# Casting all weights to bf16 ahead, and loading four of them from SyncE's queue instead of GpSimd's

## The reference, cut to what is computed

```python
def outer(x, Wq, bq, Wk, bk, Wv, bv, Wo, bo):     # x: (4, 4096, 1024), 16 heads of 64
    summary = ...                                 # mean of each 64 tokens: 64 rows a batch
    q = x @ Wq + bq; k = summary @ Wk + bk; v = summary @ Wv + bv
    attn = softmax(where(64*c <= t, q @ k.T / 8, -inf))
    return (attn @ v) @ Wo + bo

def inner_layer(x, wqkv, qs, ks, wo, lg, lb, w1, b1, w2, b2):   # 8 heads of 64, window 512
    q, k, v = split(shift_token(x) @ wqkv, 3)     # wqkv: 1024 x 1536
    q, k = rotary(l2norm(q) * qs, l2norm(k) * ks)
    x = x + local_attention(q, k, v) @ wo         # wo: 512 x 1024
    h = layernorm(shift_token(x)) * lg + lb
    a, g = split(h @ w1 + b1, 2)                  # w1: 1024 x 5460
    return x + (a * gelu(g)) @ w2 + b2            # w2: 2730 x 1024

x = x + outer(layernorm(x), ...)
x = x + inner(layernorm(x), ...)                  # inner: two inner_layers, one after the other
```

## Time and profile before

| | us |
|---|---|
| median of 3 runs | 9315.27 |
| lowest, highest | 9222.44, 9327.99 |
| the profiled execution | 9222.44 |
| its span, slowest core | 9220.9 |
| its cores | 9170.8 to 9220.9 |

### The profile page before, as it was taken

The page is one execution under the profiler, slowest core; times in us unless marked ns, Lnnn a source line. Parts: engine busy times, 40 slices in busy tenths (PEclk is TensorE's granted clock), DMA queues, the critical chain, the costliest instruction groups (busy, mean ns, idle before and its releaser), DMA issues.

```text
span 9220.9 us, 69626 instructions; the slowest of 8 cores (9170.8 to 9220.9 us)
## 1 busy us (share of the span) xinstructions
PE 3090.8 (34%) x13385; PEld 1298.5 (14%) x13385; DVE 2255.6 (24%) x4885; ACT 2991.8 (32%) x3389; POOL 456.1 (5%) x818
## 2 busy tenths in 40 slices
PE   0123233233332222222225676333221212125554
PEld 0001111101111111111112232211111110112222
DVE  0253434332322222222221111111222222221110
ACT  0232222244443333433332232344333333332121
POOL 0010000100000000000000000000000000000000
PEclk9996566555555555555558888555555555557887
DMA  9422010210100000000004554300000000003454
GB/s 108 66 60 51 19 37 19 55 40 28 37 21 2 25 1 25 21 6 25 2 17 95 120 109 97 71 14 21 6 20 6 25 2 25 2 17 95 81 102 74
DMA packets 599496, 379.98 MB, mean 41 GB/s; under 512 B 484341, under 2 KB 523509, under 8 KB 597966
## 3 DMA queue, kind: packets, MB, share of 16 engines
q1 hardware_dynamic: 550894, 234.72, 11.0%
q0 software_dynamic: 48192, 140.80, 8.1%
HBM read 343.69 MB, written 123.99 MB: 51 GB/s over the span
## 4 chain that ended last, share of the span: by engine, by line
PE 28%; ACT 26%; issue 15%; DVE 14%; DMA 5%; DVEq 5%; another core or an unknown queue 3%; SPq 1%; POOL 1%; ACTq 0%; POOLq 0%
PE pb L1986 6%; ACT L1761 4%; ACT L1723 4%; DMA wA<-w1b 3%; PE pb L2040 3%; ACT kband L1723 3%; DVE stat_s L1711 3%; PE pb L1775 3%; DVEq L230 2%; PE pQ L1750 2%; ACT pcm L1761 2%; DVE so L1698 2%; PE pb L1681 2%; PE pb L1449 2%
## 5 line engine op out<-in xcount | busy, mean ns | idle before, releaser
L1986 PE MATMUL pb<-xgb,wA 128*128 128x512 bf16 (+2 forms) x3520 | 775.5, 383 | 502.8 <-DMA wA<-w1b 449.8
L1723 ACT ACT_TABLE_LOAD x304 | 390.0, 1283 | 1694.1 <-DVE stat_s L1711 1694.1
L1750 PE MATMUL pQ<-identb,kband 128*128 128x128 bf16 x1520 | 210.0, 302 | 1685.5 <-DVE kband L1739 1685.5
L501 ACT ACT_TABLE_LOAD x264 | 338.7, 1283 | 1143.6 <-DMA xfr<-xf 514.4
L2004 ACT ACT_TABLE_LOAD x220 | 282.3, 1283 | 1232.7 <-PE pb L1986 1232.7
L1761 ACT ACT_TABLE_LOAD x304 | 390.0, 1283 | 576.5 <-PE pQ L1750 576.5
L1698 DVE SCALAR_TENSOR_TENSOR so<-pb,maskt 128x512 f32<-128x512 f32 x304 | 210.2, 692 | 1256.8 <-PE pb L1683 1256.8
L1775 PE MATMUL pb<-pcm,vI 128*64 128x128 bf16 x1520 | 246.7, 286 | 730.8 <-ACT pcm L1761 730.8
L1986 PEld LDWEIGHTS pb<-xgb,wA 128*128 128x128 bf16 (+1 forms) x3520 | 344.3, 104 | 933.8 <-issue 617.9
L513 PE MATMUL pb<-xbr,onescol 128*1 128x512 bf16 (+2 forms) x264 | 149.1, 565 | 774.7 <-POOL xbr L492 768.1
L1750 PEld LDWEIGHTS pQ<-identb,kband 128*128 128x128 bf16 x1520 | 137.8, 131 | 1853.9 <-issue 1853.9
(11 more groups left out here) (161 smaller groups left out, 5199.1 us busy)
## 6 DMA issues: line engine op xcount, KB each, us to landing
wA<-w1b SPq DMA_DIRECT2D x420, 256.0 KB, 4.2
w1b<-w1i POOLq DMA_DIRECT2D x8, 2730.0 KB, 141.5
mid_sp<-fsp POOLq DMA_DIRECT2D x72, 256.0 KB, 7.9
xfr<-mid_sp SPq DMA_DIRECT2D x72, 256.0 KB, 6.5
xfr<-xf SPq DMA_DIRECT2D x64, 256.0 KB, 5.9
xfr<-xw SPq DMA_DIRECT2D x48, 256.0 KB, 9.2
x_sp<-fsp POOLq DMA_DIRECT2D x48, 256.0 KB, 7.8
xfr<-x_sp SPq DMA_DIRECT2D x48, 256.0 KB, 4.9
```

Source lines behind the costliest of these rows:

```text
L501: tk = bd.inc("ln_sq", sc.activation(out=xsq[c % 2][:, 0:w], in_=xf32_bufs[c][1], func=AF.Square))
L1723: tk = bd.inc("expf", sc.activation(out=pn[:, 0:640], in_=so[:, 0:640], func=AF.Exp, bias=stat[:, h:h + 1], accum_out=zcol[:, h:h + 1]))
L1750: i = t.transpose(pbf[0][:, 128 * j:128 * (j + 1)], pn[:, 128 * j:128 * (j + 1)], ident)
L1986: i = t.matmul(bank[0:wdt, 0:gw], ws[:, wdt * c:wdt * (c + 1)], xgb[c][:, slot * 513:slot * 513 + gw], start=(c == 0), stop=(c == NCHUNK - 1))
```

## The change

Every weight that is still loaded as f32 gets a bf16 copy in HBM, made by `p0_wcast` ahead of the old casts: Wk, Wv, Wq, Wo, and for each layer wqkv and wo. That is 28 more copies of 256 rows, on GpSimd's queue. The token `tok_wpc` covers all 58 copies. The loads into `wA` and `wB` then read the copies, and SyncE issues them instead of GpSimd, after a wait for `tok_wpc`. They take their place in SyncE's list of blocks. `wqkv_ld` and `wo_ld` now wait for all their buffers first, and then issue all their DMAs. The reads of `wA` and `wB` in outer attention are entered in the read lists.

```diff
+    wqkb_sp = [nc.dram_tensor(f"wqkb{l}", [DIM, 1536], BF16, kind="Internal").ap()
+               for l in range(2)]
+    wo2b_sp = [nc.dram_tensor(f"wo2b{l}", [512, DIM], BF16, kind="Internal").ap()
+               for l in range(2)]
+    woutb_sp = {nm: nc.dram_tensor(f"wb_{nm}", [DIM, DIM], BF16,
+                                   kind="Internal").ap()
+                for nm in ("wq", "wk", "wv", "wo")}
...
         def p0_wcast(g):
+            for nm, srcw in (("wk", Wk_d), ("wv", Wv_d), ("wq", Wq_d),
+                             ("wo", Wo_d)):
+                for r in range(0, DIM, 256):
+                    tk = bd.inc("wpc", g.dma_start(
+                        out=woutb_sp[nm][r:r + 256, :],
+                        in_=srcw[r:r + 256, :]), 16)
             for l in range(2):
+                for r in range(0, DIM, 256):
+                    tk = bd.inc("wpc", g.dma_start(
+                        out=wqkb_sp[l][r:r + 256, :],
+                        in_=wqkv_d[l][r:r + 256, :]), 16)
+                for r in range(0, 512, 256):
+                    tk = bd.inc("wpc", g.dma_start(
+                        out=wo2b_sp[l][r:r + 256, :],
+                        in_=wo2_d[l][r:r + 256, :]), 16)
                 for r in range(0, DIM, 256):
...
         def stream_w(dram, dest, tag, ncols=DIM, nchunk=NCHUNK):
-            def ld(g):
+            def ld(sy):
+                bd.wait(sy, tok_wpc0)
                 for c in range(nchunk):
-                    bd.wait_r(g, dest[c])
+                    bd.wait_r(sy, dest[c])
                 for c in range(nchunk):
-                    tk = bd.inc(f"wc_{tag}", g.dma_start(
+                    tk = bd.inc(f"wc_{tag}", sy.dma_start(
...
-            bd.GP(ld)
+            bd.SY(ld)
...
-        tok_wk = stream_w(Wk_d, wA, "wk")
-        tok_wv = stream_w(Wv_d, wB, "wv")
+        tok_wk = stream_w(woutb_sp["wk"], wA, "wk")
+        tok_wv = stream_w(woutb_sp["wv"], wB, "wv")
...
-        tok_wq = stream_w(Wq_d, wA, "wq")
-        tok_wo = stream_w(Wo_d, wB, "wo")
+        tok_wq = stream_w(woutb_sp["wq"], wA, "wq")
+        tok_wo = stream_w(woutb_sp["wo"], wB, "wo")
...
                     if p == 7:
                         for c in range(NCHUNK):
                             bd.did_read(xgb[c], tk)
+                            bd.did_read(wA[c], tk)
...
+                        for c in range(NCHUNK):
+                            bd.did_read(wB[c], tk)
...
-            def wqkv_ld(g, l=l, tag=tag):
+            def wqkv_ld(sy, l=l, tag=tag):
+                bd.wait(sy, tok_wpc)
                 for c in range(NCHUNK):
-                    bd.wait_r(g, wA[c])
-                    tk = bd.inc(f"wqk{tag}", g.dma_start(
+                    bd.wait_r(sy, wA[c])
+                    bd.wait_r(sy, wB[c])
+                for c in range(NCHUNK):
+                    bd.inc(f"wqk{tag}", sy.dma_start(
                         out=wA[c][:, 0:1024],
-                        in_=wqkv_d[l][128 * c:128 * (c + 1), 0:1024]), 16)
+                        in_=wqkb_sp[l][128 * c:128 * (c + 1), 0:1024]), 16)
+                    tk = bd.inc(f"wqk{tag}", sy.dma_start(
+                        out=wB[c][:, 0:512],
+                        in_=wqkb_sp[l][128 * c:128 * (c + 1), 1024:1536]), 16)
+                for c in range(NCHUNK):
                     bd.wrote(wA[c], tk)
...
-            bd.GP(wqkv_ld)
+            bd.SY(wqkv_ld)
...
-            def wo_ld(g, l=l, tag=tag):
+            def wo_ld(sy, l=l, tag=tag):
+                bd.wait(sy, tok_wpc)
                 for c in range(4):
-                    bd.wait_r(g, wB[c])
-                    tk = bd.inc(f"wol{tag}", g.dma_start(
+                    bd.wait_r(sy, wB[c])
+                for c in range(4):
+                    tk = bd.inc(f"wol{tag}", sy.dma_start(
                         out=wB[c][:, 0:1024],
-                        in_=wo2_d[l][128 * c:128 * (c + 1), 0:1024]), 16)
+                        in_=wo2b_sp[l][128 * c:128 * (c + 1), 0:1024]), 16)
+                for c in range(4):
                     bd.wrote(wB[c], tk)
-            bd.GP(wo_ld)
+            bd.SY(wo_ld)
```

More of the change, by code:

```diff
@@ L443, in build_program @@
         tok_wpc = ("wpc", bd.counts["wpc"])
+        tok_wpc0 = tok_wpc
         def p0_init(v):
@@ L1295, in build_program @@
             ffng = groups((ffn0, WIN))
-            def wqkv_ld(g, l=l, tag=tag):
+            def wqkv_ld(sy, l=l, tag=tag):
+                bd.wait(sy, tok_wpc)
                 for c in range(NCHUNK):
-                    bd.wait_r(g, wA[c])
-                    tk = bd.inc(f"wqk{tag}", g.dma_start(
+                    bd.wait_r(sy, wA[c])
+                    bd.wait_r(sy, wB[c])
+                for c in range(NCHUNK):
+                    bd.inc(f"wqk{tag}", sy.dma_start(
                         out=wA[c][:, 0:1024],
-                        in_=wqkv_d[l][128 * c:128 * (c + 1), 0:1024]), 16)
+                        in_=wqkb_sp[l][128 * c:128 * (c + 1), 0:1024]), 16)
[3 more added lines that the diff above has]
+                for c in range(NCHUNK):
                     bd.wrote(wA[c], tk)
-                    bd.wait_r(g, wB[c])
-                    tk = bd.inc(f"wqk{tag}", g.dma_start(
-                        out=wB[c][:, 0:512],
-                        in_=wqkv_d[l][128 * c:128 * (c + 1), 1024:1536]), 16)
                     bd.wrote(wB[c], tk)
-            bd.GP(wqkv_ld)
+            bd.SY(wqkv_ld)
             tok_wqkv = (f"wqk{tag}", bd.counts[f"wqk{tag}"])
```

## The result

| | before | after |
|---|---|---|
| median of 12 runs, us | 9244.6 | 9380.2 |
| lowest, highest | 9222.4, 9359.2 | 9361.9, 9442.3 |
| profiled execution, span | 9220.9 | 9360.7 |

The ratio of after to before is 1.0138, with a 95% interval of 1.0108 to 1.0167. The changed kernel is 1.4% slower, some 130 us: a clear loss, and inside the 2% that were called hard to tell. The forecast was 1.7% and 9470 us; most of the distance in us is the base, since the median of the first three runs (9315.3) stands 71 us above that of twelve.

The account below looks back on a forecast made before the run. The kernel was taken as a chain of waits, its first 316 us lasting as long as the casts. Terms 136 + 12 - 6 - 21 + 34 = +155 us on the median 9315.3 gave 9470 us, range 9370 to 9520 (8 in 10).

Parts of the forecast that it names:

- What bounds the start: Start: the first 316 us last as long as the casts, as q0 and q1 pass packets one for one.
- Rival 3: Start: SP's queue gets longer turns, constants and x tiles pass under the casts; -81 us, 9234; chance 0.04.
- The term of the start: Start: added casts take 154 us, 18 of row and x loads hidden under them; +136 us (+130 to +154).
- outer attention +12: Summary to outer attention: x tiles wait in SP's queue behind Wq and Wo; +12 us (8 to 16).
- Layer 0's projection -6: Step to layer 0's projection: weights go first as plain bf16, first cast near 1784 us; -6 us (-10 to +2).
- Masks +17 each: Windowed attention, both layers: masks stand behind SP's wo load and its waits; +17 us each, +34 in sum.
- Layer 1 -21: Layer 0 to layer 1: SP issues wqkv early, so the activations set the end; -21 us (-15 to -24).
- Rival 1: Start: serial, constants come through only when the casts are over; +173 us, 9488; chance 0.14.
- Rival 2: Start: new casts slower than the old; at 85 GB/s they take 197 us, giving +198, 9513; chance 0.12.
- Rival 4: Masks land in time because the value matmuls end earlier than SP's lists; +121 us, 9436; chance 0.08.
- The sum: Whole kernel: 136 + 12 - 6 - 21 + 34 = +155 us, 9470 us on the median; chance 0.62.

Follow-up runs that it names:

- e3: Kernel before with the same 33.5 MB of copies cut by columns into row pieces of 2184 or 1024 bytes; ratio 0.9986 to the kernel before.
- e6: Kernel before with GpSimd waiting for the constants before it issues its 30 copies, sizes unchanged; ratio 0.9946 to the kernel before.
- e1: Kernel before plus the 28 added copies, which no load reads; ratio 1.0151 to the kernel before, median 9376 us.
- e7: The changed kernel timed once more, unaltered; ratio 1.0168 to the kernel before.
- e8: Changed kernel with wait_r issuing one wait per semaphore of a read list instead of one per token; ratio 0.9757 to the kernel before, median 9005 us.

## Why the prediction was right

- **What bounds the start** was right: the copies, through turns of one packet each. Rows 3's 1474 to 1474 became 1690 to 1692 here, and e3 and e6 show these turns from two more sides. The Trainium skill's turn of 9 to 17 descriptors (DMA: Bandwidth & Descriptors, section "Queues, rings and completion order") doesn't appear in any of these counts if a packet of the profile is one descriptor. In e6 the packets of the x load were single rows; whether a row is a descriptor the runs can't show. Rival 3 fell.
- **The term of the start**: +136 forecast, +138.8 measured (+136.4 and +136.6 in e1 and e7). Its parts: the copies' last packet ended at 473.4 us (median of the cores; 314.8 before), 158.6 later where 154 were forecast; constants at 390, measured 381 to 390 by core. From the copies' end to the first cast it was 24.4 us before and is 4.6 now, so 19.8 us of rows and x load are hidden, 18 in the forecast. The x load was issued at 424 us, ran beside the copies for 49, and only 5 us of its 54 came after them. So the two parts were 4.6 and 1.8 us off, to opposite sides.
- **The move's terms**: outer attention +12, measured +12.8: 10.9 of them to the first cast, which alone was forecast, and 1.9 to the first q matmul, for which I had no term and have no cause. Layer 0's projection -6, measured -6.4. Masks +17 each, measured +17.0 and +16.6 (14.9 core by core). The parts, forecast and read: mask issued 14 us after the matmul and 13.2, landing 6 and 5.2; e8 confirms the 6 us of lists in it. Layer 1 -21, measured -22.2.
- **Rival 1** (a serial start, +173) fell, as the constants did pass before the copies' end. **Rival 2** fell: the new copies ran at 108 and 109 GB/s like the old. **Rival 4** fell with the mask as releaser.
- **The sum**: +155 forecast; the terms measured sum to +157, and the time moved by +128 (ratio) to +136 (medians) in twelve runs, and by +155 (ratio) or +124 (medians) in six later ones. The interval of the twelve, +100 to +154, ends just below the terms. In the two traces the difference lies in outer attention and the last stage, which by e3 and e6 vary as much between executions; for the medians its place isn't shown. The step that made the forecast 90 us too high in absolute time was taking the median of three runs as the base: 71 of the 90.
- **What I did not see**: the list walks. I priced a wait at 0.05 us and used it for SyncE's lists alone. VectorE walks lists as well: some 150 us of them stood before L2059, as "issue", within a sum of 562.6. All lists together were worth some 350 to 400 us, more than the 262 us (by its ratio) of moving the copies.

## What to carry to other kernels

A preparation that nobody needs for a long time is free only where nobody waits: ask of each copy when its first reader comes (here 3 ms later) and what shares its queues and turns until then; moved out of the start, 309 us of copies cost 4 to 12 us. A load moved to another queue brings along its waits: everything behind it in that queue now waits for its buffers too, and it is worth as much as the row that its landing releases. And "issue" in front of an instruction, repeated for each of its kind, is worth a look at how many semaphore waits the program writes there; but it can hide another wait behind them, so its sum is not what short lists give back.

## What the runs showed of the hardware

- A DMA engine took turns of one packet between the two queues, whatever the packets' length: 2.1 MB of x needed 250 us beside copies in packets of 21 to 33 KB, 44 us beside packets of 1 to 2 KB, 11 us alone. I had expected the first to be 200.
- GpSimd stopped issuing for 250.8 us with 60 copies of small pieces issued (16160 packets), went on 1.4 us after the last of these packets had ended, and the work behind them in its program stopped too. With 58 copies in large pieces (2624 packets) it didn't stop (28.78 us for all of its start).
- Each semaphore wait costs its engine about 0.05 us though it's long fulfilled: SyncE passed 119 in 6.4 us, and 11,391 fewer waits made the changed kernel 352 to 375 us faster.
